# A two-pass cross-attention kernel: where the weighted-sum matmuls of a tile stand among those of a later tile

## What is computed

```
lat = layernorm(x);  ctx = layernorm(context)
q = lat @ Wq;  k, v = split(ctx @ Wkv)
attn = softmax(clip(q @ k.T / 8, -11, 11))       # 16 heads, 128 x 12544 each
x = x + (attn @ v) @ Wo + bo
```

## Time and profile before

| | |
|---|---|
| median of 3 runs | 1081.56 us (1081.37 to 1081.64) |
| the profiled execution | 1076.75 us |
| its span | 1075.0 us |
| TensorE matmul busy | 1065.5 us |
| TensorE weight load busy | 906.0 us |
| VectorE busy | 926.8 us |
| ScalarE busy | 660.8 us |
| GpSimd busy | 171.6 us |
| granted TensorE clock, mean | 0.995 |

### The profile page before, as it was taken

The page is one execution under the profiler, slowest core; times in us unless marked ns, Lnnn a source line. Parts: engine busy times, 40 slices in busy tenths (PEclk is TensorE's granted clock), DMA queues, the critical chain, the costliest instruction groups (busy, mean ns, idle before and its releaser), DMA issues.

```text
span 1075.0 us, 18235 instructions
## 1 busy us (share of the span) xinstructions
PE 1065.5 (99%) x5510; PEld 906.0 (84%) x5510; DVE 926.8 (86%) x1321; ACT 660.8 (61%) x934; POOL 171.6 (16%) x213
## 2 busy tenths in 40 slices
PE   8999999999999999999999999999999999999998
PEld 6888888888888888888888888888888888888876
DVE  4999999999999999888888888888888888888864
ACT  4666666666666666565666666666666666666632
POOL 3233233233232232212000000000000000000000
PEclk9999999999999999999999999999999999999998
DMA  5321221221222212221151111111111111110000
GB/s 181 114 75 49 73 73 49 73 69 53 73 61 61 73 56 66 87 73 43 50 123 45 29 44 44 29 44 43 30 44 38 35 44 33 41 44 16 1 1 5
DMA packets 52509, 58.78 MB, mean 55 GB/s; under 512 B 31170, under 2 KB 32772, under 8 KB 52356
## 3 DMA queue, kind: packets, MB, share of 16 engines
q1 hardware_dynamic: 52052, 57.80, 18.5%
q10 hardware_dynamic: 432, 0.66, 0.2%
HBM read 58.20 MB, written 0.13 MB: 54 GB/s over the span
## 4 chain that ended last, share of the span: by engine, by line
PE 98%; DVE 1%; ACT 0%; issue 0%; POOL 0%; DVEq 0%; POOLq 0%
PE wide L458 25%; PE wide L459 25%; PE wide L460 25%; PE wide L499 17%; PE wide L516 1%; PE wide L523 1%; PE wide L530 1%; PE wide L509 0%; PE wide L545 0%; PE wide L551 0%; PE wide L538 0%; PE wide L744 0%; PE wide L680 0%; PE wide L668 0%; PE wide L726 0%; PE wide L662 0%
## 5 line engine op out<-in xcount | busy, mean ns | idle before, releaser
L816 ACT ACTIVATE ex<-wide,c_rstd 128x512 f32<-128x512 f32 x392 | 270.3, 690 | 201.3 <-PE wide L460 200.2
L458 PE MATMUL wide<-qk_hi,d_hi 128*128 128x512 f32 x784 | 305.2, 389 | 0.0
L460 PE MATMUL wide<-qk_hi,d_lo 128*128 128x512 f32 x784 | 305.0, 389 | 0.0
L459 PE MATMUL wide<-qk_lo,d_hi 128*128 128x512 f32 x784 | 305.0, 389 | 0.0
L1018 DVE TENSOR_TENSOR ph<-ex,ph 128x1024 fp32r<-128x1024 f32 x195 | 239.0, 1225 | 73.7 <-ACT ph L823 73.6
L823 ACT CAST ph<-ex 128x1024 fp32r<-128x1024 f32 x195 | 205.3, 1053 | 148.6 <-DVE ex L1000 148.6
L1027 DVE TENSOR_TENSOR den_all<-den_all,ex 128x1024 f32<-128x1024 f32 x193 | 234.6, 1215 | 0.0
L499 PEld LDWEIGHTS wide<-ph,vhl 128*128 128x128 f32 x1568 | 212.7, 190 | 16.6 <-DVE ph L1018 2.1
L499 PE MATMUL wide<-ph,vhl 128*128 128x256 f32 x1568 | 218.9, 282 | 0.0
L458 PEld LDWEIGHTS wide<-qk_hi,d_hi 128*128 128x128 f32 x784 | 147.1, 188 | 31.8 <-DVE qk_lo L1032 0.3
L459 PEld LDWEIGHTS wide<-qk_lo,d_hi 128*128 128x128 f32 x784 | 147.2, 188 | 30.8
(11 more groups left out here) (163 smaller groups left out, 636.0 us busy)
## 6 DMA issues: line engine op xcount, KB each, us to landing
t_all<-in_ctxT_dram SPq DMA_DIRECT2D x98, 384.0 KB, 3.1
x_pair<-in_ctx_dram SPq DMA_DIRECT2D x49, 256.0 KB, 2.7
diff<-sig_all SPq DMA_DIRECT2D x194, 0.5 KB, 1.9
wkv<-in_Wo_dram SPq DMA_DIRECT2D x2, 1024.0 KB, 10.1
wq<-in_Wq_dram SPq DMA_DIRECT2D x2, 512.0 KB, 7.7
wkv<-in_Wv_dram SPq DMA_DIRECT2D x2, 512.0 KB, 6.5
wkv<-in_Wk_dram ACTq DMA_DIRECT2D x1, 512.0 KB, 4.7
wkv<-in_Wk_dram SPq DMA_DIRECT2D x1, 512.0 KB, 3.6
```

Of the source, the lines that this page charges most:

```text
L458: pe.matmul(dst, hi, mhi, start=start, stop=False)
L459: pe.matmul(dst, hi, mlo, start=False, stop=False)
L460: return pe.matmul(dst, lo, mhi, start=False, stop=stop)
L816: act.activation(ex[b][:, c * HC:(c + 1) * HC, :], sc_bank[c][:, :].rearrange("p (h q) -> p h q", h=HC), ACT.Exp, scale=c_rstd[s4][:, b:b ...
```

## The change

On TensorE, a turn now is: the values and scores of a tile g+1 together with the sums of tile g-1. The first value matmul is followed by one sum, the second by one, and so on for six; then the seventh sum, the first score matmul and the eighth sum; then the other eleven scores. All waits of the values and the sums stand in front of the first value matmul: `s_dlo`, `s_vlo` of g, `s_plo` of g-1. The sums of a tile used to stand behind the scores of the tile after it, which is directly ahead of the place where they are mixed in now. Before the end, the sums of the last but one tile stand alone (`sums_alone`), and those of the last go out in two halves as before. At the start of pass 1 ScalarE's and VectorE's saves move behind the cast and behind L1018 of that tile.

```diff
+            def tile(p, gp, s, b, sums=None):
                 g = 2 * gp + b
                 if b == 0:
                     pe.wait_ge(s_dlo, gp + 1)
-                if not first:
-                    pe.wait_ge(s_vlo, g)
+                pe.wait_ge(s_vlo, g)
+                steps = iter(())
+                if sums:
+                    sum_b, start, stop, saved = sums
+                    pe.wait_ge(s_plo, g - 1)
+                    if saved:
+                        pe.wait_ge(s_save, saved)
+                    steps = sum_products(sum_b, start, stop, range(MH))
+                for ins in value_products(p, s, b):
+                    next(steps, None)
                 ins.then_inc(s_v, 1)
+                for c in range(CH):
                     pe.wait_ge(s_exp, CH * (g - 1) + c + 1)
+                    products = score_products(p, s, b, c)
+                    if c == 0 and sums:
+                        next(steps)
+                        next(products)
+                        next(steps).then_inc(s_pv, 1)
+                    for ins in products:
+                        pass
+                    ins.then_inc(s_scores, 1)
...
-            def weighted_sum(gp, b, start, stop, saved=0, ended=False):
...
-                    if not ended:
-                        values(next_p, gp + b, slot(p, phase, b, 2), 1 - b)
-                        for c in range(CH):
-                            scores(next_p, gp + b, slot(p, phase, b, 2), 1 - b, c)
                     if ended:
+                        sums_alone(1 - b, 2 * gp)
                         pe.wait_ge(s_vlo, ALL)
                         pe.wait_ge(s_den, ALL - 1)
                         denominators(v_bank, den[1], True, False)
                         pe.wait_ge(s_clip, ALL + 1)
                         denominators(v_bank, ex[b], False, True)
-                    weighted_sum(gp, b, first, last, saved=p * MH if first else 0, ended=ended)
+                        last_sums(b)
+                    else:
+                        start = static and i == 0 and b == 1
+                        stop = static and i == 0 and b == 0
+                        sums = None if begun else (1 - b, start, stop, p * MH if start else 0)
+                        tile(next_p, gp + b, slot(p, phase, b, 2), 1 - b, sums)
...
-                    if static and p > 0 and i == 0 and b == 0:
-                        save_part(p - 1)
                     if more1:
                         p_high(g, b, used=not begun)
                     else:
                         p_high_last(g, b)
+                    if static and p > 0 and i == 0 and b == 0:
+                        save_part(p - 1)
...
-                    if static and p > 0 and i == 0 and b == 0:
-                        save(p - 1)
...
                         p_low(g, b)
                     else:
                         p_low_last(g, b)
+                    if static and p > 0 and i == 0 and b == 0:
+                        save(p - 1)
```

More of the change, by code:

```diff
@@ L455, in _, with value_products, score_products, sum_products @@
         def _(pe):
[L456 to L462, removed]
+            def value_products(p, s, b):
+                keys, cols = slice(b * P, (b + 1) * P), slice(p * IH, (p + 1) * IH)
+                for k in range(KD):
+                    for n, (hi_lo, w) in enumerate(((d_hi, wv_hi), (d_hi, wv_lo), (d_lo, wv_hi))):
+                        yield pe.matmul(v_bank[:, :], hi_lo[s][:, k, keys], w[:, k, cols], start=(k == 0 and n == 0),
+                                        stop=(k == KD - 1 and n == 2))
+            def score_products(p, s, b, c):
+                cols = slice((p * CH + c) * CW, (p * CH + c + 1) * CW)
+                keys = slice(b * P, (b + 1) * P)
+                for k in range(KD):
+                    for n, (hi_lo, w) in enumerate(((d_hi, qk_hi), (d_hi, qk_lo), (d_lo, qk_hi))):
+                        yield pe.matmul(sc_bank[c][:, :], hi_lo[s][:, k, keys], w[:, k, cols], start=(k == 0 and n == 0),
+                                        stop=(k == KD - 1 and n == 2))
+            def sum_products(b, start, stop, ms):
+                for m in ms:
+                    for a in range(2):
+                        yield pe.matmul(acc[m][:, a, :, :], vhl[b][:, 2 * m + a, :, :].rearrange("p n d -> p (n d)"),
+                                        ph[b][:, place(m, a), :, :], start=start and a == 0, stop=stop and a == 1)
+            def first_tile_values():
+                pe.wait_ge(s_dlo, 1)
+                *_, ins = value_products(0, 0, 0)
+                ins.then_inc(s_v, 1)
+            def first_tile_scores(c):
+                *_, ins = score_products(0, 0, 0, c)
+                ins.then_inc(s_scores, 1)
+            def tile(p, gp, s, b, sums=None):
                 g = 2 * gp + b
@@ L473, in values @@
+                for ins in value_products(p, s, b):
+                    next(steps, None)
                 ins.then_inc(s_v, 1)
-            def scores(p, gp, s, b, c, first=False):
-                g = 2 * gp + b
-                if not first:
+                for c in range(CH):
                     pe.wait_ge(s_exp, CH * (g - 1) + c + 1)
[L480 to L485, removed]
@@ new lines, in tile, with sums_alone @@
+                    if c == 0 and sums:
[4 more added lines that the diff above has]
+                        pass
+                    ins.then_inc(s_scores, 1)
+            def sums_alone(b, g):
+                pe.wait_ge(s_plo, g + 1)
+                for ins in sum_products(b, False, False, range(MH)):
+                    pass
+                ins.then_inc(s_pv, 1)
@@ L506, in denominators, with last_sums @@
+            def last_sums(b):
+                for c in range(CH):
+                    pe.wait_ge(s_plo, ALL + c)
+                    for n, ins in enumerate(sum_products(b, False, True, CHUNK_M[c])):
+                        if n % 2 == 1:
+                            ins.then_inc(s_acc, 1)
             def denominators(dst, by_head, start, stop):
@@ L586, in _ @@
                 pe.wait_ge(s_qklo, KD * (c + 1))
-                scores(0, 0, 0, 0, c, first=True)
+                first_tile_scores(c)
             pe.wait_ge(s_wv[0], 16)
@@ L593, in _ @@
             pe.wait_ge(s_wvlo, KD)
-            values(0, 0, 0, 0, first=True)
+            first_tile_values()
             pe.wait_ge(s_qT, CH + 1)
@@ L601, in pair @@
                     next_p = p + 1 if static and i == PAIRS - 1 and b == 1 else p
-                    first = static and i == 0 and b == 0
-                    last = static and i == PAIRS - 1 and b == 1
-                    ended = last and p == PASSES - 1
+                    ended = next_p == PASSES
+                    begun = static and p == 0 and i == 0 and b == 0
                     if next_p > p and not ended:
```

1 line of the change is left out of this document (removed).

## The result

| | before | after |
|---|---|---|
| median of the runs on one chip | 1081.46 us (4 runs, 1080.22 to 1081.64) | 1090.69 us (4 runs, 1089.76 to 1091.97) |
| the profiled execution, its span | 1076.75 us, 1075.0 us | 1091.05 us, 1089.3 us |
| TensorE matmul busy | 1065.5 us | 1079.5 us |

The ratio is 1.0089 (95% interval 1.0071 to 1.0106): 9.2 us slower on the medians. The forecast was 1081.2 us in 1076.5 to 1086.5, so the time lies outside the range.

A forecast was written before the change was run, and what follows sets the result against it. TensorE, busy 1065.5 of 1075.0 us, was taken to bound the kernel. Order -2.2, moved wait +0.75 and pass border +1.1 gave -0.4 us together on the median 1081.56: 1081.2 us, range 1076.5 to 1086.5.

The forecast's parts named there:

- term A: Matmul order on TensorE: each matmul keeps its steady-row time, -0.02 us a tile in 112 tiles, -2.2 us.
- worst bound: In term A: every short matmul 0.12 us, eight longs behind one 0.235, a tile 5.11 us, +0.05.
- rival 4: TensorE order: alternation costs +0.05 us in 112 tiles (+5.6), +3.3 in 82 more, about 1092 with Term B and Term C; 8%.
- Two readings: In term A: shorts stay 0.12 and values lose their extra (5.04 us), or shorts 0.113, longs behind them 0.232 (5.03).
- Tiles it counts in: term A counts in 16 late tiles of pass 0 and 96 of pass 1; VectorE paces pass 0 until then.
- Term B: Head of a pass 0 tile: TensorE waits for VectorE's low values, latency 0.28 us, slips once; +0.75 us for the pass.
- Term C: Between the passes: saves behind the casts delay the first values of pass 1, +1.1 us, once.
- Costed at nothing, pass 1: Value wait in pass 1 hidden by 0.07 us a pair; later `s_pv` moves ScalarE's values by 0.15 at most.
- The rule of the Trainium skill: Gap of columns / 2.4 + 2.5 ns, load hidden behind the short matmul: order on TensorE is worth nothing.
- best bound: In term A: every short matmul 0.113 us, every long 0.2267, a tile 4.985 us, -0.075.
- rival 1: TensorE order: alternation reaches -0.075 us a tile, or half of the way: 1075 us, half of it 1078; 25%.

The follow-up runs named there:

- r8_first: The changed kernel with a tile's eight sums in one row ahead of the values, its waits and saves kept: 1083.16 us against 1081.05 before, ratio 1.0014.
- r8_first_late: As r8_first, but with the waits for `s_dlo` and `s_vlo` put back behind the sums: 1081.75 us against 1080.3 before, ratio 1.0011.
- s1: The changed kernel with single sums between two long matmuls, two sums last, the values' wait behind the first sum: 1171.42 us against 1078.49 before.
- bank_alt: The kernel before with the six values and first six scores alternating, all 512 columns, each writing another bank: 1083.71 us against 1080.3 before.
- wide_alt: The changed kernel with each sum 512 columns wide instead of 256, in the same alternation, output another one: 1241.51 us.

## Why the prediction was wrong

**The step that failed is term A:** "each matmul keeps what it takes in its own steady row", -0.02 us a tile. It measured +0.0467 (5.1067 against 5.0600), near the worst bound of +0.05, and in every tile of both passes. That bound counted eight longs right behind a short one, where the order has seven; with seven it would have been 5.10, so the measured slot lies above it. What came is rival 4, which had 8%: it gave +5.6 and +3.3 with B and C, about 1092; the median is 1090.69. Two readings agreed at 5.03 to 5.04, and I took their agreement for evidence, though both let either the short or the long ones go without the extra that each pays. The row to believe was the 0.235 of a long one behind shorts. Against it I argued that those stood behind eight short ones; after shows that one is enough. The scores at 228 to 236 behind other scores were in neither bound, though before had the like, in the fourth and fifth value behind its row. Why a change of length costs this stays open; the runs show where it falls, and that equal lengths, in any order, don't have it.

**Tiles it counts in.** The forecast let A count in 112 tiles, since VectorE was to pace the rest. Where alternation costs, this turns: TensorE's own 5.107 us are longer than VectorE's round, and the cost is paid in nearly all tiles. Rival 4 had this right (5.11 against 5.07).

**Term B, the moved wait in pass 0: the direction right, the size and a part of the mechanism not.** In r8_first against r8_first_late it is +1.36 us, where +0.75 was forecast. The latency was taken too large. From the timelines of VectorE and TensorE where r8_first truly waits:

```profile
207.99 0.74 DVE L1016 SCALAR_TENSOR_TENSOR vhl<-wide,c_rstd,vhl 128x512 fp32r<-128x512 f32 x1
...
208.78 1.01 PEld L477 LDWEIGHTS wide<-ph,vhl 128*128 128x128 f32 x8 [0.26 <-DVE vhl L1016]
...
209.84 0.40 PE L461 MATMUL wide<-wv_hi,d_hi 128*128 128x512 f32 x1
```

L1016 ends at 208.73, and the value matmul starts 0.95 + 0.16 behind that, with the row of sums between, not 0.95 + 0.28. The missing part is the sentence that VectorE, running late, finds the exp done. It does so in one tile of two only (215.15 against 214.84, then 219.93 against 219.90). Why one slot in each hardware-loop turn is 0.10 longer still was not tested. In after itself B has nearly vanished: its slots in pass 0 are 5.1096 us beside 5.1067 in pass 1, 0.003 more, since the slower TensorE gives VectorE its lead back. So the 7.4 us that r8_first puts down to the order is what the order costs on top of a wait that it hides; terms A and B don't add.

**Term C, the border: right.** Forecast +1.1. The table's +1.13 spans three tiles, with the alternation in them; the one long slot itself is 6.09 us where its neighbours have 5.11, so +0.98 (+1.05 in r8_first, which has no alternation). With the slot's start at t = 539.13, the timelines of after by engine:

```profile
541.92 1.20 ACT L862 COPY osum<-wide 128x256 f32<-128x256 f32 x4
...
543.01 1.41 DVE L1183 TENSOR_TENSOR osum<-osum,wide 128x256 f32<-128x256 f32 x4
...
544.34 0.74 DVE L1013 SCALAR_TENSOR_TENSOR vhl<-wide,c_rstd,vhl 128x512 fp32r<-128x512 f32 x1
...
545.15 0.19 PEld L461 LDWEIGHTS wide<-wv_hi,d_hi 128*128 128x128 f32 x1 [1.18 <-issue]
545.18 0.47 PE L461 MATMUL wide<-wv_hi,d_hi 128*128 128x512 f32 x1 [0.78 <-DVE vhl L1013]
```

The copies start at t + 2.79 (forecast 2.75), the adds at t + 3.88 (3.9), `v_low` ends at t + 5.95 (5.95), and the values start at t + 6.05 (6.2). What r8_first_late adds: 0.6 of it goes with the moved wait, 0.45 with the saves.

**Costed at nothing, pass 1: right.** No value matmul waits there; r8_first has 5.0600 to the last digit. `s_pv` at t + 2.7 did no harm to TensorE either. It moved ScalarE's half of the values (L833) to t + 2.85 in the tile shown above (803.41), 0.25 later than before, where 0.15 at most was forecast; VectorE's L1013 didn't wait for it. s1 shows that this cover has an end: with the last two sums behind the first six scores the slot is nearly half a microsecond longer.

**The rule of the Trainium skill.** Its page "TensorE: Matmul & The Clock Gate", section "Back-to-back issue gap", has no cost for the order, and its formula gives 109 and 216 ns for 256 and 512 columns. The page calls that the gap of an isolated matmul, which the prediction left out, and puts a stream of pairs of load and matmul at about 131 ns for 512 columns. The runs show 120 and 227 in steady rows, each matmul with its load, so neither figure holds here. They show 5.107 us alternating and 5.060 in a row, where the formula's sum is one for all orders. For the order of unequal matmuls the measurement decides against it.

**The range.** It ended at 1086.5 and left out rival 4 and the full best bound. The two bounds of A, -0.075 and +0.05, are 0.125 us a tile apart, 24 us over 194 tiles; I had no row between them and gave the worse end 8%. A range that took in both ends of an unmeasured cost would have held the time. (In rival 1, half of the way in term A gives 1079.2 us, not 1078; nothing else hangs on that.)

## What to carry to other kernels

When TensorE has no idle time, look at the distances between starts around each change of length, up to seven places behind it, and put both the gain and what is paid back into one sum before you call one of them free. In this kernel one row of the eight short matmuls, or pairs of them with two long ones between, cost least (5.060 and 5.053 us a tile); pairs with three long ones between, threes and fours cost 5.067 to 5.080, and one at a time 5.107. A wait moved ahead of its cover can be priced only with the whole loop that it closes, and it can be hidden again by the very slowness that comes with it: in r8_first it cost 1.36 us, in after next to nothing.

## What the runs showed of the hardware

- Distance of this kernel's matmuls, which have a weight load each, at granted clock 1.00: 120 and 227 ns for 256 and 512 columns in steady rows (a line through the two is columns / 2.4 + 13 ns); 147 and 175 for 320 and 384 columns, taken in the alternation alone.
- With unequal lengths the sum is more than that of the steady ones: for eight of 256 among 18 of 512 a tile took 5.107 us one at a time, 5.073 in two rows of four, 5.060 in one row, 5.053 in four pairs with two long ones between (steady rows would give 8 x 120 + 18 x 226.7 = 5.04). With all at 512 columns it is 5.8933 in either order.
- The extra isn't in the neighbour alone: the five longs behind a row take 233 236 228 233 231 ns. It follows neither the bank (bank_alt) nor the source of the weights (wide_alt), and it doesn't vanish at 320 or 384 columns. What causes it stays open.
- The last 50 us, at a granted clock of 0.77 to 0.87, vary by 6 us between executions of the same work (45.1 to 51.2), more than most effects studied here.
